# In the last stage of a graph and mixture-of-experts kernel, GpSimd sums the row pairs of two of nine token groups

## The reference, cut to what matters

```python
x = x + gnn(layernorm(x), ...)                 # earlier stages
def ffn(x, ...):
    topk_vals, topk_idx = top_k(x @ gate_w + gate_b, 2)
    topk_w = softmax(topk_vals)
    moe = sum over the 2 chosen experts of topk_w * (relu(x @ w1 + b1) @ w2 + b2)
    y = x + moe
    return (y - mean(y)) / sqrt(var(y) + 1e-5) * gamma + beta
x = x + ffn(layernorm(x), ...)
```

## Time and profile before

| what | value |
|---|---|
| median of 3 runs | 886.51 us (880.44 to 890.98) |
| profiled execution, its time | 891.48 us |
| profiled execution, its span | 889.7 us |
| TensorE busy | 744.3 us (84%) |
| VectorE busy | 671.5 us (75%) |
| ScalarE busy | 475.8 us (53%) |
| GpSimd busy | 280.9 us (32%) |

### The profile page before, as it was taken

One profiled execution on the slowest core, in us unless ns is written; L12 is line 12 of the kernel. 1 busy time (PEld: TensorE's weight loads), 2 busy tenths in 40 slices (PEclk: granted clock), 3 DMA queues, 4 the chain that ended last, 5 costly groups with the idle time before them and its releaser, 6 DMA issues.

```text
span 889.7 us, 21308 instructions
## 1 busy us (share of the span) xinstructions
PE 744.3 (84%) x6322; PEld 641.1 (72%) x6322; DVE 671.5 (75%) x1830; ACT 475.8 (53%) x1199; POOL 280.9 (32%) x313
## 2 busy tenths in 40 slices
PE   4555788888885776898899999999999999998893
PEld 3555355555555766777787899999998899997682
DVE  6999799999953687877765677777776677775497
ACT  5995677877726666744433344444444344443253
POOL 9400000000000457777744345445432222223010
PEclk9999699999987576569999999999999999999797
DMA  9840444545535934359988899999899999993999
GB/s 268 232 149 1 129 152 145 171 154 166 158 100 208 230 122 141 126 176 305 303 240 251 236 275 265 261 263 267 265 270 329 278 261 262 266 265 115 353 312 199
DMA packets 156241, 192.82 MB, mean 217 GB/s; under 512 B 78235, under 2 KB 125262, under 8 KB 153036
## 3 DMA queue, kind: packets, MB, share of 16 engines
q1 hardware_dynamic: 128056, 113.07, 45.3%
q10 hardware_dynamic: 14440, 47.37, 16.1%
q0 software_dynamic: 13632, 31.03, 11.0%
HBM read 151.05 MB, written 40.34 MB: 215 GB/s over the span
## 4 chain that ended last, share of the span: by engine, by line
PE 47%; DVE 25%; SPq 11%; issue 10%; DMA 4%; ACT 2%; DVEq 0%; ACTq 0%; POOL 0%; POOLq 0%
PE PS L1300 16%; PE PS L1312 15%; DVE W L1361 10%; SPq L723 7%; DVE W L1427 5%; PE PS L1338 4%; DVE W L1392 3%; DMA R<-xs 3%; PE PS L1190 2%; PE PS L1205 2%; PE PS L1218 2%; SPq L726 2%; SPq L320 1%; PE PS L1094 1%; PE PS L1058 1%
## 5 line engine op out<-in xcount | busy, mean ns | idle before, releaser
L1300 PEld LDWEIGHTS PS<-R,W 128*128 128x128 f32 x1808 | 218.9, 192 | 27.2 <-DVE R L1646 20.4
L1300 PE MATMUL PS<-R,W 128*128 128x128 f32 x1808 | 223.0, 276 | 16.2 <-DVE R L1646 14.4
L996 ACT ACTIVATE R<-PS,b1T 128x128 f32<-128x128 f32 x350 | 102.9, 367 | 226.6 <-PE PS L1300 224.6
L1312 PE MATMUL PS<-W,R 128*128 x904 | 216.0, 383 | 0.0
L612 POOL DMA_INDIRECT ys<-W,R x113 | 109.9, 973 | 234.6 <-DVE W L1698 229.2
L1312 PEld LDWEIGHTS PS<-W,R 128*128 128x128 f32 x904 | 165.1, 193 | 18.1
L1361 DVE TENSOR_TENSOR W<-R,W 128x3136 bf16<-128x3136 bf16 (+1 forms) x104 | 156.8, 1562 | 1.1 <-PE PS L1074 1.1
L894 ACT ACTIVATE W<-PS 128x1024 f16<-128x1024 f32 x104 | 106.3, 1023 | 37.9 <-PE PS L1094 33.3
L605 POOL DMA_INDIRECT xs<-W,slot_i x98 | 100.5, 1025 | 79.3 <-DVE slot_i L1526 51.0
L1094 PE MATMUL PS<-W,table 114*128 114x512 f16 x208 | 66.6, 404 | 25.9 <-DVE W L1392 25.5
L597 POOL MEMSET R<- 128x261 f32 x1 | 0.3, 317 | 227.1 <-PEq L1136 227.1
(11 more groups left out here) (267 smaller groups left out, 1034.7 us busy)
## 6 DMA issues: line engine op xcount, KB each, us to landing
W<-in_L_ffn_w ACTq DMA_DIRECT2D x89, 512.0 KB
W<-in_L_ffn_w SPq DMA_DIRECT2D x40, 512.0 KB, 8.7
W<-key_rows SPq DMA_DIRECT2D x26, 784.0 KB
R<-xs SPq DMA_DIRECT2D x113, 130.5 KB
W<-ys SPq DMA_DIRECT2D x4, 2048.0 KB, 12.6
R<-xs SPq DMA_DIRECT2D x224, 32.0 KB
XH<-in_x SPq DMA_DIRECT2D x6, 896.0 KB, 11.7
W<-xs SPq DMA_DIRECT2D x116, 32.0 KB
```

The source lines that it names most:

```text
L996: last = act.activation(HT3[:, u, j, :], up_out(u, j), ACT.Relu, bias=b1T[:, ds(e, 1), j])
L1300: last = nc.tensor.matmul(up_out(u, j), W1S[b][:, k, j * P:(j + 1) * P], XT3[:, u, k, :], start=(k == 0), stop=(k == 1))
L1312: last = nc.tensor.matmul(PS[:, 6 * u, 0:C], HT3[:, u, j, :], wt2(e * W2COLS, j), start=(j == 0), stop=(j == 3))
```

## The change

For groups 4 and 6 (`FPOOL`), GpSimd adds a token's second row to its first in place in the load buffer, and TensorE skips these groups. VectorE's statistics and ScalarE's normalisation of these groups read the load buffer and not PSUM. GpSimd sums group 4 ahead of its three out-adds and group 6 between the first and the second of them. The buffer of group 4 can be loaded again (for group 8) only when ScalarE has read it.

```diff
+FPOOL = (4, 6)
...
         def y_sum(g, j):
+            if g in FPOOL:
+                return y_two[g % YBUFS][:, j, 0, :]
             return PS[:, 4 * (g % 2) + j // 2, (j % 2) * C:(j % 2 + 1) * C]
+        def wait_sum(eng, g, j):
+            if g in FPOOL:
+                eng.wait_ge(y_pooled, on_pool(g) + j + 1)
+            else:
+                eng.wait_ge(y_summed, FG[g][0] - on_pool(g) + j + 1)
...
+                def sum_rows(g):
+                    u = g % YBUFS
+                    pool.wait_ge(y_in[u], y_loads(g))
+                    for j in range(FG[g][1]):
+                        nc.gpsimd.tensor_tensor(y_two[u][:, j, 0, :], y_two[u][:, j, 0, :], y_two[u][:, j, 1, :], ALU.add
+                                                ).then_inc(y_pooled, 1)
+
+                sum_rows(FPOOL[0])
                 pool.wait_ge(base_stored, 16 * len(FADD))
                 for g in FADD:
                     t, n = FG[g]
+                    if g == FADD[1]:
+                        sum_rows(FPOOL[1])
                     pool.wait_ge(scaled_ready, g + 1)
                     pool.dma_start(out[t * P:(t + n) * P, :].rearrange("(t p) c -> p t c", p=P),
...
                     if g >= YBUFS:
-                        sp.wait_ge(y_summed, sum(FG[g - YBUFS]))
+                        if g - YBUFS in FPOOL:
+                            sp.wait_ge(hat_ready, sum(FG[g - YBUFS]))
+                        else:
+                            wait_sum(sp, g - YBUFS, FG[g - YBUFS][1] - 1)
...
                 for g in range(NFG):
+                    if g in FPOOL:
+                        continue
                     t, n = FG[g]
                     pe.wait_ge(y_in[g % YBUFS], y_loads(g))
...
-                        dve.wait_ge(y_summed, FG[g][0] + min(j | 1, n - 1) + 1)
+                        wait_sum(dve, g, min(j | 1, n - 1))
```

More of the change, by code:

```diff
@@ L488, in build @@
         y_summed = sem("y_summed")
+        y_pooled = sem("y_pooled")
         def up_out(u, j):
@@ L493, in y_sum, with on_pool @@
         def y_sum(g, j):
+            if g in FPOOL:
+                return y_two[g % YBUFS][:, j, 0, :]
             return PS[:, 4 * (g % 2) + j // 2, (j % 2) * C:(j % 2 + 1) * C]
+        def on_pool(g):
+            return sum(FG[i][1] for i in FPOOL if i < g)
+        def wait_sum(eng, g, j):
[3 more added lines that the diff above has]
+                eng.wait_ge(y_summed, FG[g][0] - on_pool(g) + j + 1)
         def y_loads(g):
```

## The result

The changed kernel takes 892.08 us (median of 20 runs), the kernel before 886.85 us (median of 20 runs). The ratio is 1.0057, with a 95% interval of 1.0037 to 1.0077: the change costs 5.1 us, between 3.3 and 6.8. The forecast was 890.5 us, +4.0.

What follows compares the result with a forecast made beforehand. The prediction took a nearly full VectorE as the bound, with 1.2 us to gain. The third out-add's landing, 4.0 us late (3.0 of the chain, 1.0 for the second transfer), on the median 886.5 gave 890.5 us, range 884 to 897.

Steps and rivals of the forecast that it cites:

- What a faster sum can give: Behind group 3 VectorE waits for TensorE only 0.22 and 0.96 us, so at most 1.2 us can be gained.
- Group 5 waits for group 3's normalisation: TensorE stands still from about 846.3 to 853.2, so group 5 starts only 0.3 us earlier.
- The lower clock in group 5: After its pause TensorE restarts at the lower clock in group 5, losing 1.8 to 4.1 us; 2.2 taken.
- Contention in group 4: VectorE's operations wait for GpSimd's additions in group 4, 0 to 2.2 us; one addition, 0.7 us, taken.
- Contention in group 6: GpSimd's eight additions (5.9 us) are held up by VectorE's two-input operations falling among them (2.4 us).
- The end of the sums of group 6: GpSimd's sums of group 6 end at 869.2 or 872.2, without or with the 3.0 us ahead of the first out-add.
- the hold: Unexplained 3.0 us ahead of the first out-add on GpSimd; both ends kept, gone or 3.0 as before.
- VectorE's last pair of group 6: VectorE's last pair of group 6 starts between 869.6 and 872.2, 1.7 to 4.3 us late; 3.0 taken.
- The out-adds as the last to arrive: VectorE's products of group 8 wait for the third out-add's landing, 1.4 to 6.9 us late; 4.0 taken.
- the additions stretch: Rival: VectorE's work holds GpSimd up; at 1.5 us an addition the third out-add is +10.5, 897; chance 0.14.
- additions of over 1.3 us: Sign of being wrong, in GpSimd's sums: additions last over 1.3 us, where near 0.73 was expected.
- hidden: Rival: 3.0 us hold gone, additions fit VectorE's one-input work, out-adds keep their times; -1.2 to +1.5, chance 0.22.

Runs made afterwards that it cites:

- e11: Changed kernel with group 6's sums ahead of the first out-add and TensorE doing matmuls on other data in skipped groups; +2.5 us over the kernel before, ratio 1.0028.
- e2: Changed kernel with GpSimd summing group 6 only, TensorE summing group 4 again; +8.2 us over the kernel before, ratio 1.0092.
- e4: Changed kernel with TensorE doing 16 matmuls on other data where it skips groups 4 and 6; +5.1 us over the kernel before, ratio 1.0058.
- e5: Kernel before, TensorE summing all groups, plus GpSimd's sixteen additions written to a spare place that nobody reads; +5.5 us, ratio 1.0062.
- e1: Changed kernel with GpSimd summing group 4 only, TensorE summing group 6 again; +3.9 us over the kernel before, ratio 1.0044.
- e7: Changed kernel with a GpSimd wait behind each addition and TensorE matmuls on other data in skipped groups; +4.2 us over the kernel before, ratio 1.0047.
- e9: Changed kernel with a wait behind each addition, matmuls on other data in skipped groups, and group 6's sums ahead of the out-adds; +5.3 us over the kernel before.
- e10: Changed kernel with one more GpSimd wait, behind the first addition of group 6; +6.3 us over the kernel before, ratio 1.0071.
- e3: Changed kernel with GpSimd waiting for each addition's semaphore before the next; +3.9 us over the kernel before, ratio 1.0044.
- e6: Changed kernel with GpSimd summing group 6 ahead of the first out-add; +1.3 us over the kernel before, ratio 1.0015.

## Why the prediction was right

The forecast, 890.5 us and no change within 1%, held: 892.08, +5.1 against +4.0. The mechanism held only in part, and that the sum came so near is partly luck: the costliest step was wrong, one step was missing, and what I had as the last to arrive was not. In the profile the last products moved by 7.5 us. VectorE's delay grows to that in this order: 0.7 ahead of GpSimd's first sums, 1.0 in group 4, 1.5 in group 5, 3.8 beside the additions of group 6, 1.2 given back because the sums of group 6 were there in time, 1.7 in group 7. The steps of the prediction, with times of before moved by 3.04 us:

- **What a faster sum can give** (1.2 us, since VectorE is nearly full behind group 3). Not contradicted: no version was faster than the kernel before. It is not tested cleanly either, since in e11, where the most costs are gone, an out-add sets the end.
- **Group 5 waits for group 3's normalisation.** Right. That ended at 848.16 + 3.76 = 851.92, 1.7 us late, and TensorE paused for 7.56 us. Of the 1.7, 0.7 were there ahead of GpSimd's first sums: the clock rose later after the first pause (0.50 granted at 828 to 831, against 0.61 at the same place before), in code that the change leaves alone.
- **The lower clock in group 5** (2.2 taken). 32 records in 8.80 us against 7.16, 1.6 us, a little under my bounds of 1.8 to 4.1. The step was right, but I left out that group 7 follows a pause too. It cost VectorE 1.49 us, and this step was missing.
- **Contention in group 4** (0.7 taken). 0.59 - 0.17 and 1.29 - 0.68, 1.0 us. Right in kind, and near in size.
- **Contention in group 6.** This step failed. I let GpSimd wait for VectorE's two-input operations, from the earlier trace rows. In the changed kernel VectorE waited, 3.70 us at an operation of 0.17, and 5.6 us in e2, e4 and e5. The early rows show GpSimd held up by VectorE's unbroken work; the other direction is not in them, as I had noted, and I priced it for group 4 alone, and in a rival at one addition for each operation.
- **The end of the sums of group 6** (46.3 to 49.2 us into the stage, with or without the hold). 49.6. The hold was there (857.14 to 860.16, 3.0 us), and the time came out nearly right: GpSimd's last two additions met VectorE's products after all, and one took 3.5 us. Still, VectorE never waited for a sum of group 6, as I had expected it to.
- **VectorE's last pair of group 6** (1.7 to 4.3 late). Its statistics of group 6 ended 5.9 us late, since the products of group 4 came behind the additions and not among them.
- **The out-adds as the last to arrive.** Wrong for the changed kernel. The third landed 64.9 us into the stage, 5.1 late and inside the range of 1.4 to 6.9. But VectorE came 2.5 us after it, with everything in its own chain late by 7.5 us. Where VectorE loses less it does set the end (e1, e7, e9 and e11).

The Trainium skill (SBUF — State Buffer, section "SBUF: two separate sides") gives the lock to whichever instruction starts first, for that whole instruction. Group 4's rows agree: 0.59 and 1.29 us, one addition waited for each time. In group 6 the measurement goes beyond the rule: VectorE was shut out until six additions had ended, and eight in e2, where each was started well ahead of the end of another. e10 shows that a single wait ends it. That the early start itself keeps the lock is my reading of GpSimd's recorded spans, which are rough, and is not shown.

The rival "the additions stretch" gave GpSimd's side 1.3 us an addition as the point from which the kernel is slower by 1%. The eight took 8.27 us, 1.03 each. I had also named additions of over 1.3 us as a sign of being wrong, and six of those of group 6 are recorded at 1.4; but one began every 0.68 us, so VectorE lost the time there and not these six. The rival "hidden" fell with the hold and the lockout.

## What to carry to other kernels

Work moved from a full TensorE to an idle engine gains at most what the next engine's waits can give back, and that is to be read behind the place of the move, per stage. Before putting a row of GpSimd additions beside VectorE, ask in both directions who waits: a row that starts right behind a GpSimd DMA shut VectorE out for six to eight additions, and one semaphore wait behind its first addition ended that, though the time did not fall with it (e10). Where several costs hide behind each other, removing one gives back little, so cost each alone in the kernel before, as e5 does, and follow each engine's own rows, as in e11.

## What the runs showed of the hardware that was not expected

- VectorE's small operations can wait for six to eight GpSimd additions in a row: 3.70 us (changed kernel), 5.63 (e2), 5.64 (e4), 5.65 (e5), against 0.17. It happened only where the row started beside the out-add and went on without a wait; elsewhere the longest such wait was about one addition (0.93 us for an operation of 0.17, e7).
- VectorE's statistics from SBUF keep their pace beside the additions: a pair took 0.75 us in e3, and 0.76 from PSUM.
- GpSimd adds 128x256 in fp32 every 0.68 us when nothing interferes, 0.72 us for one.
- The first out-add starts 2.6 to 3.1 us after its wait ends, but at once behind additions that GpSimd does not wait for (e6, e11); the later two start some 0.3 us after theirs.
